# A two-layer attention and FFN kernel: the keys turned through the score banks, the output projections in two halves, both q projections ahead of the weighting

## Chip, cores and metric

The kernel is one program on one core of a Trainium2 chip. The metric is the device time of one execution in microseconds (us). Names of engines: PE is the matrix engine (TensorE), PEld its weight loads, DVE is VectorE, ACT is ScalarE, POOL is GpSimd.

## What is computed

The input x is 16 sequences of 64 rows of 512 numbers, in f32. Four blocks are added onto it, in this order:

```
x = x + xattn0(layernorm(x), ctx)   # 32 q heads, 8 kv heads, rotary positions, softmax over 64 keys
x = x + int_ffn(layernorm(x))       # 512 -> 1376 -> 512, rounded like int8
x = x + xattn1(layernorm(x), ctx)   # 32 q heads, 8 kv heads, keys = context and x (128), q and k normed by RMS
x = x + quant_ffn(layernorm(x))     # two 512x512 products on values rounded to 8 bits
```

Both attentions are of this shape, with (in the second) a norm of q and k in place of the rotation:

```
q = x @ Wq; k = c @ Wk; v = c @ Wv          # four q heads share one kv head
p = softmax(q @ k.T / sqrt(128) (+ mask))
x += (p @ v) @ Wo
```

## The kernel before

All four blocks are written by hand: each engine has its own program in a `block`, the order of the calls is the order of the work, and counting semaphores tie the engines together. The change touches the function `attention`, which runs twice: as `att0` (rope is true, 64 keys for each sequence) and as `att1` (rope is false, 128 keys).

**Precision.** Products with weights are taken as three matmuls of rounded parts (hi*hi, lo*hi, hi*lo), by `split_product` at line 70. Nearly all matmul rows of the trace are of that line.

**Units and slots.** An attention is 32 units u = 4g + n: kv head g (0 to 7) and n from 0 to 3, where n // 2 is the half of the sequences and n % 2 the pair of q heads (out of four). The loop over u is the spine of every engine's program. One pass is called a slot here. On PE a slot has these pieces:

- `scores(u)` (line 552 in att0, 555 in att1) into the banks `sco`;
- the filling work, `filling(g, n)`: for even n four output projections `project` of an earlier half (12 matmuls each), for odd n the joint k and v projections `kv_job` of the coming half (two in att0, four in att1);
- `turn(u)` (line 570): the softmax weights are turned into the banks `att`; it waits for POOL's `normalise(u)` (line 956);
- `q_job(u + 2, 0)` and `q_job(u + 2, 1)`: the q projections of the unit after the next, 12 matmuls each;
- `weigh(u)` (585 or 595): the turned weights times V, into two `att` banks; ACT rounds these (`round_out`, 882) and DVE takes the rest (`out_low`, 758), which counts the semaphore `out_drained`; `project` reads both parts;
- behind an odd unit `turn_keys` (534): the keys of the next half are turned, one bank in att0 and two in att1, and copied by ACT (`copy_keys`, 849) to `k_cols`, which the next `scores` reads. So slots with odd n are called key slots here. The even ones are out slots.

**Banks.** PE's results have eight banks: four `proj` in a ring, two `sco`, two `att`. The jobs in `att` are numbered in order (`number_att`), and a job takes the bank of the job before the last. A turned key therefore stands in a bank in which an output of `weigh` was, and waits until DVE has drained it (`att_room`).

**The order of the q jobs.** `early_q(u)` decides it: where it is true (att0 with odd u, and u < 2), both q jobs of the slot stand in front of `weigh`. Elsewhere `turn` comes first, one q job stands between `turn` and `weigh`, and the other behind `weigh` (and, in att1, behind `turn_keys`):

```
                if early_q(u):
                    q_job(u + 2, 0)
                turn(u)
                if rope and keys_after(u):
                    turn_keys(*keys_after(u))
                q_job(u + 2, 1 if early_q(u) else 0)
                weigh(u)
                if not rope and keys_after(u):
                    turn_keys(*keys_after(u))
                if not early_q(u):
                    q_job(u + 2, 1)
```

The last two units stand behind the loop, with the last eight output projections. POOL takes the low parts of the weights (142), the rotations of att0 (942), the scaling of the keys in att1 (950) and `normalise` (956). The weights come by DMA, 256 KB each.

Of the kernel before, what the change touches and what calls it, by code (L numbers as in the profile page):

```python
# [63 lines left out]
def split_product(eng, out, terms, more=False, first=True):  # L64


    n = 0
    for lhs_hi, lhs_lo, rhs_hi, rhs_lo in terms:
        for a, b in ((lhs_hi, rhs_hi), (lhs_lo, rhs_hi), (lhs_hi, rhs_lo)):
            last = eng.matmul(out, a, b, start=(first and n == 0), stop=(n == 3 * len(terms) - 1))  # L70
            n += 1
    return last
# [260 lines left out]
def attention(nc, st, tag, rope, weights, mask=None):  # L333
# [45 lines left out]
    for i in range(TKH):  # L379
        number_att("key", 0, 0, i)  # L380
    for u in range(UNITS):
# [7 lines left out]
        new_keys = (g, 1) if n == 1 else (g + 1, 0) if n == 3 and g + 1 < NKV else None  # L389
        for i in range(TJ):  # L390
            number_att("turn", u, i)
        if rope and new_keys:
            number_att("key", *new_keys, 0)
        for i in range(2):
            number_att("out", u, i)
        if not rope and new_keys:
            for i in range(TKH):
                number_att("key", *new_keys, i)
# [7 lines left out]

    def early_q(u):
        return rope and u % 2 == 1 or u < 2

    with ExitStack() as ctx:  # L410
# [30 lines left out]
        out_rounded, out_drained = sem("out_rounded"), sem("out_drained")  # L441
        inverted, normed, v_copied = sem("inverted"), sem("normed"), sem("v_copied")
# [14 lines left out]
        def o_slice(tile, u, i):  # L457
            p, sel = u % 2, (slice(i, NBH, 2) if rope else slice(4 * i, 4 * i + 4))
            return tile[:, 2 * p:2 * p + 2, sel, :].rearrange("p g b s -> p b g s")

# [24 lines left out]
        def _(eng):  # L485
# [37 lines left out]
            def turn_keys(g, h):  # L523
                for i in range(TKH):
# [4 lines left out]
                    turned, out = att_room("key", g, h, i)  # L529
                    need(eng, turned_copied, turned)  # L530
                    need(eng, out_drained, out)
                    bank = att_bank("key", g, h, i)
                    for c in range(4):
                        last = eng.transpose(bank[:, c * P:(c + 1) * P], k_rows[:, 4 * i + c], st.ident[:])
                    last.then_inc(att_full, 1)

            def scores(u):
# [5 lines left out]
                eng.wait_ge(turned_copied, turned_by["key", g, h, TKH - 1] + 1)  # L543
# [55 lines left out]
            def project(g, h, t):  # L599
                job = proj_job["out", g, h, t]  # L600
                eng.wait_ge(w_split, weights.ready(g, C_O + GROUP - 1))
                eng.wait_ge(out_drained, 2 * (4 * g + 2 * h + 2))
                need(eng, proj_drained, job - 3)
                split_product(eng, proj[job % 4][:], [
                    (o_hi[:, a, 2 * t:2 * t + 2, :], o_lo[:, a, 2 * t:2 * t + 2, :], w_hi[:, C_O + a], w_lo[:, C_O + a])
                    for a in range(GROUP)]).then_inc(proj_full, 1)

            def fill(what):
                kv_job(*what[1:]) if what[0] == "kv" else project(*what[1:])
# [12 lines left out]
            for u in range(UNITS - 2):  # L622
                work = filling(*divmod(u, 4))
                scores(u)
# [17 lines left out]
            project(g, 0, 0)  # L642
            q_sums(u + 1)
            project(g, 0, 1)
            project(g, 0, 2)
            scores(u + 1)
            turn(u)
            project(g, 0, 3)
            weigh(u)
            turn(u + 1)  # L650
            weigh(u + 1)
            for t in range(4):
                project(g, 1, t)

        @block.vector
        def _(eng):
# [129 lines left out]
            for u in range(UNITS - 2):  # L786
# [11 lines left out]
                if early_q(u):  # L798
                    take_q(u + 2, 1)
                out_low(u)  # L800
                if not early_q(u):
# [801 lines left out]
```

## Time and profile before

| | us |
|---|---|
| median of 3 runs | 1729.88 (1729.61 to 1732.37) |
| the profiled execution, its own time | 1730.62 |
| its span in the trace | 1728.8 |
| att0, slots 2 to 29 | 497.90 |
| att1, slots 0 to 29 | 743.71 |

The mean granted clock of PE is 0.952 of full speed. The span of the trace begins with the first instruction and ends with the last; the profiled execution's own time is 1.8 us longer. The stretches of the two attentions are cut at the first matmul of `scores`, so that one slot reaches from one `scores` to the next. The order is att0 (about 50 to 617 us), the integer FFN, att1 (861 to 1645 us), the quantised FFN. "Idle before" in a row is the time in which the engine stood still just ahead of the instruction, with what released it.

### The profile page before, as it was taken

What the parts mean: (1) busy time and instruction counts of PE and PEld (TensorE: products, weight loads), DVE (VectorE), ACT (ScalarE), POOL (GpSimd) and SP (SyncE); (2) the same over time, 40 slices, a digit from 0 to 9 for tenths busy, and PEclk for the clock granted to TensorE, in tenths of its full rate; (3) what the DMA queues carried; (4) which work ended last, traced back from release to release, by engine and by line L of the source; (5) the groups of instructions that cost most, each with busy time, mean ns of one, the idle gap of its engine ahead of it and who ended that gap; (6) DMA issues with size and microseconds to landing.
All of it is one profiled execution on the core that took longest, in us unless ns stands there. A gap on an engine that the chain in (4) does not pass through costs nothing. (4 is left out here: it accounts for less than half of the span.)

```text
span 1728.8 us, 28639 instructions
## 1 busy us (share of the span) xinstructions
PE 1534.0 (89%) x11533; PEld 1306.1 (76%) x11536; DVE 973.3 (56%) x1998; ACT 600.6 (35%) x1424; POOL 564.6 (33%) x458
## 2 busy tenths in 40 slices
PE   4899999999999879987799999999999999999826
PEld 4788887888787668865688888888888788888723
DVE  6656666566655646648555444544544454455487
ACT  3212222122221224422353443435344343534345
POOL 3535444353433325522222221312222131222045
PEclk9999999999999989998899999999999999999958
DMA  5101111011110012201110010101001010100021
GB/s 163 48 27 50 35 40 37 25 58 30 38 38 25 1 55 73 69 1 57 54 38 25 25 38 1 57 6 38 26 25 38 11 52 2 38 26 1 1 73 49
DMA packets 81229, 64.43 MB, mean 37 GB/s; under 512 B 7280, under 2 KB 66928, under 8 KB 81104
## 3 DMA queue, kind: packets, MB, share of 16 engines
q1 hardware_dynamic: 80240, 62.47, 12.4%
q8 instruction: 90, 1.47, 0.4%
q14 instruction: 35, 0.29, 0.1%
q10 hardware_dynamic: 864, 0.20, 0.1%
HBM read 60.56 MB, written 2.10 MB: 36 GB/s over the span
## 5 line engine op out<-in xcount | busy, mean ns | idle before, releaser
L956 POOL TENSOR_TENSOR att_probs<-att_probs,att_total 128x512 f32<-128x512 f32 x64 | 82.9, 1295 | 566.6 <-DVE att_total L748 428.8
L142 POOL TENSOR_TENSOR att_w_lo<-att_w_raw,att_w_hi 128x512 fp32r<-128x512 f32 x160 | 205.5, 1309 | 160.2 <-ACT att_w_hi L137 160.2
L70 PE MATMUL att_proj<-att_w_hi,kv_hi 128*128 128x256 f32 x768 | 223.9, 291 | 8.7 <-PEq L223 8.6
L70 PE MATMUL att_proj<-att_w_hi,att_o_hi 128*128 128x512 f32 x512 | 205.2, 401 | 24.2 <-issue 24.2
L70 PE MATMUL att_proj<-att_w_hi,kv_lo 128*128 128x256 f32 x768 | 218.9, 285 | 0.0
L70 PE MATMUL att_proj<-att_w_lo,kv_hi 128*128 128x256 f32 x768 | 218.8, 285 | 0.0
L70 PE MATMUL att_proj<-kv_hi,att_w_hi 128*128 128x512 f32 x512 | 217.3, 424 | 0.0
L764 DVE TENSOR_TENSOR x_rows<-att_proj,x_rows 128x512 f32<-128x512 f32 x128 | 88.6, 692 | 220.4 <-PE att_proj L70 220.4
L70 PE MATMUL att_proj<-kv_hi,att_w_lo 128*128 128x512 f32 x512 | 206.9, 404 | 0.0
L70 PE MATMUL att_proj<-kv_lo,att_w_hi 128*128 128x512 f32 x512 | 206.8, 404 | 0.0
L70 PE MATMUL att_proj<-att_w_hi,att_o_lo 128*128 128x512 f32 x512 | 201.0, 392 | 0.0
L70 PE MATMUL att_proj<-att_w_lo,att_o_hi 128*128 128x512 f32 x512 | 200.6, 392 | 0.0
L70 PEld LDWEIGHTS att_proj<-att_w_hi,kv_hi 128*128 128x128 f32 x768 | 149.0, 194 | 10.8 <-issue 9.4
L871 ACT ACTIVATE att_probs_t<-att_att 128x512 f32<-128x512 f32 x96 | 54.0, 596 | 279.3 <-PE att_att L570 278.4
L70 PEld LDWEIGHTS att_proj<-att_w_hi,kv_lo 128*128 128x128 f32 x768 | 149.1, 194 | 0.0
L70 PEld LDWEIGHTS att_proj<-att_w_lo,kv_hi 128*128 128x128 f32 x768 | 149.0, 194 | 0.0
L861 ACT ACTIVATE att_probs<-att_sco,att_low,att_q_rms 128x128 f32<-128x128 f32 x256 | 113.3, 461 | 62.7 <-DVE att_low L728 62.7
L70 PEld LDWEIGHTS att_proj<-att_w_hi,att_o_hi 128*128 128x128 f32 x512 | 96.9, 189 | 45.6 <-issue 26.2
L942 POOL TENSOR_TENSOR att_q_cols<-att_turn_a,att_turn_b 128x512 f32<-128x512 f32 x64 | 86.2, 1346 | 125.5 <-DVE att_turn_b L681 125.5
L70 PEld LDWEIGHTS att_proj<-kv_lo,att_w_hi 128*128 128x128 f32 x512 | 100.3, 196 | 22.7
L70 PEld LDWEIGHTS att_proj<-kv_hi,att_w_hi 128*128 128x128 f32 x512 | 101.6, 198 | 19.3
L882 ACT ACTIVATE att_o_hi<-att_att 128x512 fp32r<-128x512 f32 x128 | 72.9, 597 | 120.4 <-PE att_att L585 101.3
(153 smaller groups left out, 2950.8 us busy)
## 6 DMA issues: line engine op xcount, KB each, us to landing
att_w_raw<-in_wq SPq DMA_DIRECT2D x64, 256.0 KB, 2.9
att_w_raw<-in_wo SPq DMA_DIRECT2D x64, 256.0 KB, 2.7
ln_stage<-in_ctx_t SPq DMA_DIRECT2D x8, 512.0 KB, 5.0
att_w_raw<-in_wk SPq DMA_DIRECT2D x16, 256.0 KB, 3.5
att_w_raw<-in_wv SPq DMA_DIRECT2D x16, 256.0 KB, 3.4
ffn_w_raw<-in_gate_t SPq DMA_DIRECT2D x10, 256.0 KB, 2.9
ffn_w_raw<-in_up_t SPq DMA_DIRECT2D x10, 256.0 KB, 3.2
ffn_w_raw<-in_down_t SPq DMA_DIRECT2D x10, 256.0 KB, 3.0
```

What stands on the lines that cost most here:

```text
L70: last = eng.matmul(out, a, b, start=(first and n == 0), stop=(n == 3 * len(terms) - 1))
L142: eng.tensor_tensor(self.lo[:, chunk], self.raw[:, n % RAW_SLOTS], raw(self.hi[:, chunk]), ALU.subtract)\
L764: eng.tensor_tensor(st.x[:, row], proj[job % 4][:], st.x[:, row], ALU.add).then_inc(proj_drained, 1)
L861: ins = eng.activation(probs[:, u % 2, b], sco[(u * SJ + i) % 2][:, c * KL:(c + 1) * KL], ACT.Exp, bias=low[:, u % 2, one], scale=q_rms[:, ...
L871: eng.activation(probs_t[:, slot], att_bank("turn", u, i)[:], ACT.Copy).then_inc(turned_copied, 1)
L882: eng.activation(o_slice(o_hi, u, i), bank, ACT.Copy).then_inc(out_rounded, 1)
L942: eng.tensor_tensor(dst, a, b, ALU.add).then_inc(rotated, 1)
L956: eng.tensor_tensor(probs[:, u % 2, 0:n], probs[:, u % 2, 0:n], total[:, u % 2, 0:n].unsqueeze(2).broadcast_to([P, n, KL]), ALU.mult)\
```

## The change

It has four parts, for both attentions.

- The keys are turned into the `sco` banks, where the next scores will go, in place of the `att` banks. The semaphores `keys_full` and `keys_copied` are new. The turning waits until the scores of all earlier units are drained (`sco_drained`), and `scores` waits for `keys_copied`. The `att` banks then hold `turn` and `weigh` alone.
- `project(g, h, t)` is cut into two half sums, p = 0 and p = 1, of six matmuls each, over two of the four heads. Half p waits for the outputs of the unit 4g + 2h + p alone. At the start of an out slot the order is t0 p0, t1 p0, t0 p1.
- `early_q` is gone. Every slot ends with q, `turn`, q, `turn_keys` (if any), `weigh`; ACT and DVE follow: both `square_q`, then `copy_keys`, then `round_out` on ACT, both `take_q` and then `out_low` on DVE.
- Behind the loop the first halves of the last four projections stand ahead of the last `turn`, the second halves at the end.

```
-            def project(g, h, t):
+            def project(g, h, t, p):
                 job = proj_job["out", g, h, t]
-                eng.wait_ge(w_split, weights.ready(g, C_O + GROUP - 1))
-                eng.wait_ge(out_drained, 2 * (4 * g + 2 * h + 2))
-                need(eng, proj_drained, job - 3)
-                split_product(...for a in range(GROUP)]).then_inc(proj_full, 1)
+                eng.wait_ge(w_split, weights.ready(g, C_O + 2 * p + 1))
+                eng.wait_ge(out_drained, 2 * (4 * g + 2 * h + p + 1))
+                if p == 0:
+                    need(eng, proj_drained, job - 3)
+                last = split_product(... for a in (2 * p, 2 * p + 1)], first=(p == 0), last=(p == 1))
+                if p == 1:
+                    last.then_inc(proj_full, 1)
...
             def turn_keys(g, h):
+                need(eng, sco_drained, SJ * key_unit(g, h))
                 for i in range(TKH):
...
-                    turned, out = att_room("key", g, h, i)
-                    need(eng, turned_copied, turned)
-                    need(eng, out_drained, out)
-                    bank = att_bank("key", g, h, i)
+                    bank = key_bank(g, h, i)
...
-                    last.then_inc(att_full, 1)
+                    last.then_inc(keys_full, 1)
...
             for u in range(UNITS - 2):
-                work = filling(*divmod(u, 4))
                 scores(u)
-                fill(work[0])
+                work = filling(*divmod(u, 4))
+                fill_first(work)
                 q_sums(u + 1)
-                for what in work[1:]:
-                    fill(what)
-                if early_q(u):
-                    q_job(u + 2, 0)
+                fill_rest(work)
+                q_job(u + 2, 0)
                 turn(u)
-                if rope and keys_after(u):
+                q_job(u + 2, 1)
+                if keys_after(u):
                     turn_keys(*keys_after(u))
-                q_job(u + 2, 1 if early_q(u) else 0)
                 weigh(u)
-                if not rope and keys_after(u):
-                    turn_keys(*keys_after(u))
-                if not early_q(u):
-                    q_job(u + 2, 1)
...
             weigh(u)
+            for t in range(4):
+                project(g, 1, t, 0)
             turn(u + 1)
             weigh(u + 1)
             for t in range(4):
-                project(g, 1, t)
+                project(g, 1, t, 1)
```

What PE has in a row at the end of a key slot of att1 (u = 9), before. In the names, `att1_` is the second attention, and the number behind a tile is its bank. Rows of line 70 with `kv1_hi` and 512 columns open a q job; the 11 rows that follow each are left out:

```order
L70 MATMUL att1_proj3<-kv1_hi,att1_w_hi 128x512 [waits att1_proj_drained,att1_w_split]
...
L595 MATMUL att1_att0<-att1_probs_t,att1_v_rows 128x128 [waits att1_turned_copied,att1_v_copied]
...
L595 MATMUL att1_att1<-att1_probs_t,att1_v_rows 128x128 [waits att1_turned_copied]
...
L534 MATMUL att1_att0<-ident,att1_k_rows 128x128 [waits att1_out_drained,att1_k_scaled]
...
L534 MATMUL att1_att1<-ident,att1_k_rows 128x128 [waits att1_out_drained,att1_k_scaled]
...
L70 MATMUL att1_proj0<-kv1_hi,att1_w_hi 128x512 [waits att1_proj_drained,att1_w_split]
...
L555 MATMUL att1_sco0<-att1_k_cols,att1_q_cols 128x128 [waits att1_sco_drained,att1_turned_copied,att1_proj_drained]
```

The same place of the changed program, from the q job behind `turn` to the first halves of the output projections (rows with `att1_o_hi`):

```order
L70 MATMUL att1_proj0<-kv1_hi,att1_w_hi 128x512 [waits att1_proj_drained,att1_w_split]
...
L529 MATMUL att1_sco0<-ident,att1_k_rows 128x128 [waits att1_k_scaled,att1_sco_drained]
...
L529 MATMUL att1_sco1<-ident,att1_k_rows 128x128 [waits att1_k_scaled]
...
L590 MATMUL att1_att0<-att1_probs_t,att1_v_rows 128x128 [waits att1_turned_copied,att1_v_copied]
...
L590 MATMUL att1_att1<-att1_probs_t,att1_v_rows 128x128 [waits att1_turned_copied]
...
L550 MATMUL att1_sco0<-att1_k_cols,att1_q_cols 128x128 [waits att1_sco_drained,att1_keys_copied,att1_proj_drained]
...
L550 MATMUL att1_sco1<-att1_k_cols,att1_q_cols 128x128 [waits att1_sco_drained]
...
L70 MATMUL att1_proj1<-att1_w_hi,att1_o_hi 128x512 [waits att1_proj_drained,att1_out_drained,att1_w_split]
...
L70 MATMUL att1_proj2<-att1_w_hi,att1_o_hi 128x512 [waits att1_proj_drained,att1_out_drained,att1_w_split]
...
L70 MATMUL att1_proj1<-att1_w_hi,att1_o_hi 128x512 [waits att1_out_drained,att1_w_split]
```

The turning of the keys no longer waits for `out_drained` and stands ahead of `weigh`; no q job is left between `weigh` and `scores`. A second bank is opened before the first sum is closed.

What ACT has in a row at the same place, before:

```order
L871 ACTIVATE att1_probs_t<-att1_att0 128x512 [waits att1_att_full]
L871 ACTIVATE att1_probs_t<-att1_att1 128x512 [waits att1_att_full]
L842 ACTIVATE att1_squares<-att1_proj3 128x8x64 [waits att1_proj_full]
L882 ACTIVATE att1_o_hi<-att1_att0 128x4x2x64 [waits att1_proj_full,att1_att_full]
L882 ACTIVATE att1_o_hi<-att1_att1 128x4x2x64 [waits att1_att_full]
L849 ACTIVATE att1_k_cols<-att1_att0,qk_norm 128x512 [waits att1_att_full]
L849 ACTIVATE att1_k_cols<-att1_att1,qk_norm 128x512 [waits att1_att_full]
L842 ACTIVATE att1_squares<-att1_proj0 128x8x64 [waits att1_proj_full]
```

And now:

```order
L878 ACTIVATE att1_probs_t<-att1_att0 128x512 [waits att1_att_full]
L878 ACTIVATE att1_probs_t<-att1_att1 128x512 [waits att1_att_full]
L849 ACTIVATE att1_squares<-att1_proj3 128x8x64 [waits att1_proj_full]
L849 ACTIVATE att1_squares<-att1_proj0 128x8x64 [waits att1_proj_full]
L856 ACTIVATE att1_k_cols<-att1_sco0,qk_norm 128x512 [waits att1_keys_full]
L856 ACTIVATE att1_k_cols<-att1_sco1,qk_norm 128x512 [waits att1_keys_full]
L889 ACTIVATE att1_o_hi<-att1_att0 128x4x2x64 [waits att1_proj_full,att1_att_full]
L889 ACTIVATE att1_o_hi<-att1_att1 128x4x2x64 [waits att1_att_full]
```

Both squares and both copies of the keys now stand ahead of the rounding of the outputs.

## Rows read from the trace of the kernel before

**Rows 1.** The page, part 1: busy us, share of the span, instructions.
```profile
PE 1534.0 (89%) x11533; PEld 1306.1 (76%) x11536; DVE 973.3 (56%) x1998; ACT 600.6 (35%) x1424; POOL 564.6 (33%) x458
```

**Rows 2.** Waits of all engines in att0: engine line waited for: us, times, longest.
```profile
PE att_proj L70 <- issue: 20.7, 15, 1.4
```

**Rows 3.** The same in att1, 850 to 1640 us.
```profile
PE att_att L534 <- DVE att_o_lo L758: 47.8, 15, 3.5
```

**Rows 4.** Stretches of slots: us; busy (instructions) PE, PEld, DVE, ACT, POOL; granted clock.
```profile
79.97:577.87 497.90, 478.34 (x3530) 401.15 (x3528) 301.34 (x505) 118.05 (x224) 215.37 (x182) 1.00 0.12 36
860.69:1604.40 743.71, 693.94 (x6074) 615.88 (x6072) 362.06 (x921) 310.34 (x885) 169.51 (x134) 0.96 0.09 26
860.69:877.63 16.94, 16.74 (x177) 15.24 (x176) 8.98 (x33) 9.38 (x27) 1.55 (x1) 1.00 0.01 2
1025.48:1054.97 29.49, 26.14 (x233) 24.17 (x232) 12.78 (x37) 11.01 (x32) 3.58 (x3) 0.88 0.01 2
...
1076.72:1103.80 27.08, 23.73 (x234) 22.04 (x233) 13.82 (x37) 14.04 (x38) 9.89 (x9) 1.00 0.14 40
1103.80:1125.55 21.75, 21.75 (x177) 18.39 (x176) 12.55 (x24) 9.18 (x26) 7.75 (x7) 1.00 0.25 74
293.34:314.42 21.08, 19.68 (x126) 15.66 (x124) 11.67 (x18) 6.63 (x12) 9.54 (x8) 1.00 0.18 51
```

**Rows 5.** PE in order of time, end of att1's key slot 7.
```profile
1043.50 1.95 PE L595 MATMUL att_att<-att_probs_t,att_v_rows 128*128 128x128 f32 x16
1048.73 1.94 PE L534 MATMUL att_att<-ident,att_k_rows 128*128 128x128 f32 x8 [3.28 <-DVE att_o_lo L758]
```

**Rows 6.** DVE, POOL and ACT in order of time, same place.
```profile
1047.90 1.28 DVE L758 TENSOR_TENSOR att_o_lo<-att_att,att_o_hi 128x512 fp32r<-128x512 f32 x2
...
1043.80 2.04 POOL L950 TENSOR_TENSOR att_k_rows<-att_k_rows,att_k_rms 128x512 f32<-128x512 f32 x2 [4.03 <-DVE att_k_rms L216]
...
1049.85 0.69 ACT L849 ACTIVATE att_k_cols<-att_att,qk_norm 128x512 f32<-128x512 f32 x1 [3.77 <-PE att_att L534]
```

**Rows 7.** PE, then DVE, in order of time, att0's slot 15 and the start of 16.
```profile
321.36 0.40 PE L70 MATMUL att_proj<-kv_hi,att_w_hi 128*128 128x512 f32 x1
...
324.12 0.60 PE L570 MATMUL att_att<-ident,att_probs 128*128 128x128 f32 x4
...
324.91 0.48 PE L70 MATMUL att_proj<-kv_hi,att_w_hi 128*128 128x512 f32 x1
...
327.81 1.16 PE L585 MATMUL att_att<-att_probs_t,att_v_rows 64*128 64x128 f32 x16
328.91 1.15 PE L552 MATMUL att_sco<-att_k_cols,att_q_cols 128*64 128x64 f32 x32
331.44 0.47 PE L70 MATMUL att_proj<-att_w_hi,att_o_hi 128*128 128x512 f32 x1 [1.38 <-issue]
...
330.05 1.29 DVE L758 TENSOR_TENSOR att_o_lo<-att_att,att_o_hi 128x512 fp32r<-128x512 f32 x2
```

**Rows 8.** POOL, then PE, in att0's key slot 17, whose scores start at 349.99.
```profile
353.52 2.99 POOL L142 TENSOR_TENSOR att_w_lo<-att_w_raw,att_w_hi 128x512 fp32r<-128x512 f32 x2
357.23 0.74 POOL L942 TENSOR_TENSOR att_k_rows<-att_turn_a,att_turn_b 128x256 f32<-128x256 f32 x1 [0.71 <-DVE att_turn_b L669]
358.06 1.04 POOL L956 TENSOR_TENSOR att_probs<-att_probs,att_total 128x512 f32<-128x512 f32 x1
...
359.68 0.60 PE L570 MATMUL att_att<-ident,att_probs 128*128 128x128 f32 x4
```

**Rows 9.** PE in order of time, att1, the end of slot 0.
```profile
875.85 1.95 PE L595 MATMUL att_att<-att_probs_t,att_v_rows 128*128 128x128 f32 x16
877.63 1.95 PE L555 MATMUL att_sco<-att_k_cols,att_q_cols 128*128 128x128 f32 x16
```

**Rows 10.** PE in order of time, the last turn of att0 and of att1.
```profile
598.33 1.11 PE L570 MATMUL att_att<-ident,att_probs 128*128 128x128 f32 x4 [3.96 <-POOL att_probs L956]
...
1627.85 1.97 PE L570 MATMUL att_att<-ident,att_probs 128*128 128x128 f32 x8 [5.22 <-POOL att_probs L956]
```

More of the change, by code:

```diff
@@ L61, with split_product @@
     pass
-def split_product(eng, out, terms, more=False, first=True):
+def split_product(eng, out, terms, first=True, last=True):
     n = 0
@@ L69, in split_product @@
         for a, b in ((lhs_hi, rhs_hi), (lhs_lo, rhs_hi), (lhs_hi, rhs_lo)):
-            last = eng.matmul(out, a, b, start=(first and n == 0), stop=(n == 3 * len(terms) - 1))
+            ins = eng.matmul(out, a, b, start=(first and n == 0), stop=(last and n == 3 * len(terms) - 1))
             n += 1
-    return last
+    return ins
 def raw(ap):
@@ L378, in attention @@
     number("q", 1, 1)
-    for i in range(TKH):
-        number_att("key", 0, 0, i)
     for u in range(UNITS):
@@ L597, in weigh, with fill_first, fill_rest @@
                     last.then_inc(att_full, 1)
-            def project(g, h, t):
+            def project(g, h, t, p):
                 job = proj_job["out", g, h, t]
-                eng.wait_ge(w_split, weights.ready(g, C_O + GROUP - 1))
-                eng.wait_ge(out_drained, 2 * (4 * g + 2 * h + 2))
-                need(eng, proj_drained, job - 3)
-                split_product(eng, proj[job % 4][:], [
-                    (o_hi[:, a, 2 * t:2 * t + 2, :], o_lo[:, a, 2 * t:2 * t + 2, :], w_hi[:, C_O + a], w_lo[:, C_O + a])
-                    for a in range(GROUP)]).then_inc(proj_full, 1)
-            def fill(what):
-                kv_job(*what[1:]) if what[0] == "kv" else project(*what[1:])
+                eng.wait_ge(w_split, weights.ready(g, C_O + 2 * p + 1))
+                eng.wait_ge(out_drained, 2 * (4 * g + 2 * h + p + 1))
+                if p == 0:
+                    need(eng, proj_drained, job - 3)
+                last = split_product(eng, proj[job % 4][:], [
+                    (o_hi[:, a, 2 * t:2 * t + 2, :], o_lo[:, a, 2 * t:2 * t + 2, :], w_hi[:, C_O + a], w_lo[:, C_O + a])
+                    for a in (2 * p, 2 * p + 1)], first=(p == 0), last=(p == 1))
+                if p == 1:
+                    last.then_inc(proj_full, 1)
+            def fill_first(work):
+                if work[0][0] == "kv":
+                    kv_job(*work[0][1:])
+                    return
+                project(*work[0][1:], 0)
+                project(*work[1][1:], 0)
+                project(*work[0][1:], 1)
+            def fill_rest(work):
+                for i, what in enumerate(work[1:]):
+                    if what[0] == "kv":
+                        kv_job(*what[1:])
+                        continue
+                    if i:
+                        project(*what[1:], 0)
+                    project(*what[1:], 1)
             for j in range(KVH):
@@ L797, in _ @@
                 take_q(u + 2, 0)
-                if early_q(u):
-                    take_q(u + 2, 1)
+                take_q(u + 2, 1)
                 out_low(u)
-                if not early_q(u):
-                    take_q(u + 2, 1)
             u, g = UNITS - 2, NKV - 1
```

43 lines of the change are left out of this document (18 added, 25 removed).

## The prediction, made before the changed kernel was run

> **What bounds the kernel now.** Part 1 of the page comes first: PE is busy for 89% of the span, no other engine for more than 56% [rows 1]. So what counts is where PE stands still or runs slowly. I then read the waits of PE by stage, and then the order of time around each.
>
> In att0 one wait repeats: 15 times 1.4 us, 20.7 us in all, ahead of an output projection [rows 2]. The order of time shows which: `scores(16)` starts at 328.91, takes 1.09 us (the step from `weigh` to `scores`, 327.81 to 328.91, is as long), and the first projection starts at 331.44, because `out_low` on DVE runs from 330.05 to 331.34 [rows 7]. Start to start the loss is 1.44 us, a little more than the modelled 1.38. It stands in every out slot from 2 to 30: the key slot ahead of it has `weigh` last. An out slot takes 21.08 us, and the granted clock is 1.00 over all of slots 2 to 29 [rows 4].
>
> In att1 PE waits for DVE's `out_low` before it turns keys: 47.8 us in 15 places [rows 3]. `weigh` starts at 1043.50; 16 matmuls of 0.106 us end at 1045.20; the turning starts at 1048.73, when DVE, which began `out_low` only at 1047.90, has drained the first bank [rows 5, 6]. The loss is 3.53 us. Then comes the second price: the 8 transposes take 1.94 us, where 8 of att0 take 0.79 (324.12 to 324.91) [rows 7], since the clock has fallen to the lower of its two levels (1.2 GHz, not 2.4). Slot 7 takes 29.49 us at clock 0.88, slot 9, without the lower level, 27.08 at 1.00 [rows 4]. Out slots take 21.75 at 1.00, with PE busy throughout. What the clock costs in all comes out of the same rows: slot 0 of 16.94, slot 1 of at most 21.3 (slot 0, 0.8 for its keys, 3.5 of stall), and 14 pairs of 27.08 + 21.75 make 721.9; the stretch took 743.71. So 21.8 us are the clock's.
>
> **The change, part by part.** The sum is made against the profiled execution's own time, 1730.62 us, which is 0.74 above the median.
>
> *Keys in the score banks, ahead of `weigh`.* The wait for `out_drained` goes. What the turning waits for instead: the scores drained (the softmax of the same slot needs them, done before `turn`), and the keys scaled. In slot 7 POOL scales them from 1043.80 to 1045.84 [rows 6]. `weigh` began at 1043.50, behind one q job; now the filling is followed by q, turn, q, so the turning begins one q job (2.76 us) later, at 1046.3: 0.4 us to spare. Each clean key slot then costs 27.08 - 3.53 = 23.55 us. Behind the transposes stand `weigh` and `scores`, and `scores` needs the copies. With T the start of the turning, ACT squares q until T + 0.9 (0.2 us of lag and 0.69, as its copy of a bank takes) and copies twice in 0.69: T + 2.3. PE comes to `scores` at T + 0.8 + 1.8 = T + 2.6 (`weigh` takes 1.78, rows 9). In att0 it is one copy, T + 1.35 against T + 0.4 + 1.1 = T + 1.5 [rows 6, 7, 9]. Both are hidden, by 0.3 and 0.15 us; I price them at nothing and keep 0.3 us in 30 slots, 9 us, for the upper end.
>
> *Half sums.* In att0 `out_low` ends 2.43 us after `weigh` does (331.34 against 328.91) [rows 7]. The first matmul that needs it now stands behind `scores` and two halves: 1.1 + 2 x 1.38 = 3.9 us. So the 1.44 us go, with 1.4 to spare. In att1 no q job stands between `weigh` and the projections any more, so the wait could be new there. In slot 7 `weigh` would end at 1046.3 + 0.8 + 1.8 = 1048.9, and the second half of t0 comes 1.8 + 2.8 us later, at 1053.5. DVE ends `out_low` at 1049.18, plus a `take_q` of 0.7 that now stands before it: 1049.9. Hidden by 3.5 us. The number of matmuls is the same, and sums in two banks at once cost nothing that the rows show.
>
> *Both q jobs ahead of `weigh`.* `weigh` and `scores` become neighbours in 28 more slots. Each change from the large to the small products and back costs a little: the q job right behind the filling takes 321.36 to 324.12 = 2.76 us, the one behind small ones 324.91 to 327.81 = 2.90 [rows 7]. I take 0.14 in att0 and 0.1 in att1. DVE begins the next scores behind `out_low`, about where it began them before.
>
> It has a cost in att0. With n = 0 POOL splits four chunks after ACT has rounded them behind `round_out`. In slot 17 that ended at 356.51, 6.5 us after `scores` began at 349.99, and `normalise` ran from 358.06 to 359.10, just ahead of `turn` at 359.68 [rows 8]. `scores` now begins one q job earlier against that chain. From the end of `weigh`: three roundings on ACT at 0.6, 1.8; four splits and a rotation of the same size on POOL at 1.3 to 1.5 (2.99 for two), some 6.9; the rotation of keys 0.74 and 1.04 for `normalise`: 10.5 us, against 9.7 at which `turn` arrives (359.68 - 349.99). ACT and POOL overlap a little, so I take a new wait of 0.5 us in 7 slots, 3.5 us; bounds 0 and 1.0 each.
>
> *The tails.* PE stood idle 3.96 and 5.22 us before the last turns, for POOL [rows 10]. The four first halves (5.5 us) fill that, but they need `out_low` of the unit just weighed, so a stall of 2 to 3.5 us appears ahead of them. I take 2 us gained in each; bounds 0 and 9.2 together.
>
> *The clock.* In att0 idle stretches of 1.44 us never brought the lower level in 28 slots. If att1 has no idle of 3.5 us left I expect the full clock there too. The 21.8 us are then gone as well.
>
> **The sum.** att1, slots 0 to 29, was 743.71. Now slot 0: 16.94 as before; slot 1 is slot 0 plus 8 transposes, 17.8 (rounded up); 14 out slots of 21.65; 14 key slots of 23.45. That makes 666.1, so 77.6 saved. att0: 14 x (1.44 + 0.14) + 1.44 - 3.5 = 20.1. Tails 4. In all 101.7: 1730.62 - 101.7 = 1628.9, and 1628.2 as a median.
>
> **A rule against it.** Rows 9 show `weigh` and `scores` as neighbours at full speed, 16 matmuls in 1.78 us, twice over: 3.5 us of small products without a fall. In a key slot the turning now stands before them, 4.4 us. The Trainium skill, TensorE: Matmul & The Clock Gate, Part 4: PE-mode transpose, says that a transpose doesn't count as PE-busy in the way a matmul does. By that rule the turned keys lengthen a quiet stretch, and the lower level stays in the key slots. No row has turning, weighting and scores in a row, so none refutes it; rival 1 is what it would come to.
>
> **The rivals.**
> 1. *The clock keeps falling in key slots*, because 4.4 us of small products work as the idle stretch did. For it: the new length. Against it: rows 9, and clock 1.00 in att0, where `weigh`, `scores` and 1.44 us of idle stood together. Price: the 21.8 us of now, giving 1650; with slot 7's 29.49 - 27.08 = 2.4 in each of 15 slots 36, giving 1664.
> 2. *Small waits take the place of the large one*: the copies or the scaled keys come later than the margins of 0.15 to 0.4 us. At 0.8 us in 30 slots, 24 us: 1652.
> 3. *Slower.* Turning now stands in front of `weigh`, so a late key holds `weigh`, and with it `round_out`, `out_low` and the projections. POOL would have to deliver 101.7 / 30 = 3.4 us behind PE in each key slot to eat up the gain, that is 3.8 later than in slot 7; from there it decides. At 4 us: 120 us, 1748. Against it: nothing ahead of the scaling on DVE or POOL moves.
> 4. *No change*: the stalls only move, as to the second half of t0. Margins of 1.4 and 3.5 us speak against it. About 1730.
>
> **Chances.** The forecast 0.76, rival 1 0.10, rival 2 0.10, rival 3 0.02, rival 4 0.02. So faster 0.96, same 0.02, slower 0.02; 0.2% is about what a measurement of this kernel can tell. The lower end: tails 9.2 (-5), no wait in slot 17's kind (-3.5), and the waits for `normalise` in the out slots gone too (-3): 1617. The upper end: tails 0 (+4), 1.0 us in that kind (+3.5), copies late (+9), and half a step of rival 1: 1648.
>
> **What would show it.** Right: no row of PE waiting for `out_low` ahead of turned keys; key slots of att1 near 23.5 and out slots near 21.65; out slots of att0 near 19.5; granted clock 1.00 in both; a small wait of `turn` for POOL in att0's slots 5, 9, 13 and so on. Wrong: clock below 0.98 in att1 (rival 1); PE waiting for ACT's copies or POOL's keys (rival 2), or for `out_low` in the second half of t0 (rival 4).

## The result and the profile after

The changed kernel takes 1623.77 us, the median of 4 executions (1622.98 to 1625.15); the kernel before took 1729.74 on the same chip (4 executions, 1728.78 to 1732.37). The ratio is 0.9386, with a 95% interval of 0.937 to 0.9402: faster by 6.1%. The forecast was 1628 (1617 to 1648), 4 us too high. The profiled execution took 1622.98 us with a span of 1621.2, against 1730.62 and 1728.8 before. (Of the four executions of the experiment q_order_only below, one of 1729.89 us had a mean clock of 0.89 where the others had 0.96 to 0.97; its figures there leave it out.)

Part 1 of the page after, beside [rows 1]: PE's busy time fell by 39 us although it executes the same number of matmuls, and its share rose from 89 to 92%.

```profile
PE 1495.1 (92%) x11533; PEld 1287.9 (79%) x11536; DVE 980.7 (60%) x1998; ACT 596.4 (37%) x1424; POOL 564.6 (35%) x458
```

The stretches after, with the columns of [rows 4] (from and to, length; busy PE, PEld, DVE, ACT, POOL with instructions; granted clock; DMA share; GB/s). In order: slots 2 to 29 of att0, slots 0 to 29 of att1, att1's slot 0, one of its key slots and one of its out slots; then from att0 the out slot 16, and the key slots 17 and 19:

```profile
79.36:556.30 476.94, 473.71 (x3531) 403.47 (x3529) 299.74 (x505) 119.62 (x224) 214.69 (x182) 1.00 0.13 37
835.68:1498.51 662.83, 662.62 (x6073) 596.87 (x6072) 370.97 (x921) 304.70 (x885) 170.09 (x134) 1.00 0.10 29
835.68:852.62 16.94, 16.74 (x178) 15.26 (x177) 9.00 (x33) 9.38 (x27) 1.55 (x1) 1.00 0.00 1
1026.42:1049.56 23.14, 23.14 (x235) 21.92 (x234) 13.89 (x38) 12.76 (x36) 8.63 (x7) 1.00 0.16 46
1049.56:1071.31 21.75, 21.75 (x179) 18.47 (x178) 13.81 (x25) 10.12 (x28) 9.08 (x7) 1.00 0.25 74
317.50:336.73 19.23, 19.23 (x128) 15.81 (x126) 10.54 (x17) 2.32 (x4) 3.62 (x3) 1.00 0.00 1
336.73:351.91 15.18, 14.72 (x132) 12.97 (x130) 10.67 (x21) 5.65 (x11) 10.44 (x9) 1.00 0.24 71
371.12:385.63 14.51, 14.51 (x132) 13.04 (x130) 10.26 (x21) 3.57 (x7) 6.79 (x7) 1.00 0.12 37
```

The second row is the main reading: PE busy for 662.62 of 662.83 us at clock 1.00, where [rows 4] had 693.94 of 743.71 at 0.96. The two long rows of waits [rows 2, 3] are gone. What PE still waits for in att0 (75 to 560 us) is one row; in att1 (830 to 1500 us) it is 0.2 us, once:

```profile
PE att_att L565 <- POOL att_probs L958: 3.2, 7, 0.5
```

Where the 107.6 us between the two profiled spans came from, by the starts of the slots in the two traces: att1's slots 0 to 29 80.9 (743.71 - 662.83), att0's slots 2 to 29 21.0 (497.90 - 476.94), the stretch from att0's slot 30 to att1's slot 0 3.4 (282.82 to 279.38), what follows att1's slot 29 1.7 (124.4 to 122.7), and 0.6 ahead of slot 2.

PE in order of time in the changed kernel, att1's key slot 11 (the counterpart of [rows 5]), and behind it ACT's row of copies and DVE's first `out_low`:

```profile
1091.79 1.03 PE L529 MATMUL att_sco<-ident,att_k_rows 128*128 128x128 f32 x8
1092.66 1.95 PE L590 MATMUL att_att<-att_probs_t,att_v_rows 128*128 128x128 f32 x16
1094.45 1.95 PE L550 MATMUL att_sco<-att_k_cols,att_q_cols 128*128 128x128 f32 x16
1096.15 0.48 PE L70 MATMUL att_proj<-att_w_hi,att_o_hi 128*128 128x512 f32 x1
...
1092.48 1.26 ACT L856 ACTIVATE att_k_cols<-att_sco,qk_norm 128x512 f32<-128x512 f32 x2
...
1094.38 0.69 DVE L768 TENSOR_TENSOR att_o_lo<-att_att,att_o_hi 128x512 fp32r<-128x512 f32 x1
```

Turned keys, `weigh` and `scores` fill 1091.79 to 1096.15, 4.36 us, each starting as the one before ends. The copies end at 1093.74, 0.7 us ahead of the scores that read them. POOL had scaled the keys at 1091.68, only 0.1 us ahead of the turning where the prediction had 0.4, but the q job ahead of the turning takes its usual 2.82 us, so nothing waited. `out_low` starts 0.07 us before `scores` do and nothing on PE asks for it yet.

### The profile page after: what moved, and what is told of

Same layout as the page of the kernel before. It is cut to its first block and busy times, and to the rows that moved or that the text cites. A ratio compares the mean times of both kernels' runs of the same rounds, so it can differ in the third digit from the quotient of the medians.

```text
span 1621.2 us, 28750 instructions
## 1 busy us (share of the span) xinstructions
PE 1495.1 (92%) x11533; PEld 1287.9 (79%) x11536; DVE 980.7 (60%) x1998; ACT 596.4 (37%) x1424; POOL 564.6 (35%) x458
## 5 line engine op out<-in xcount | busy, mean ns | idle before, releaser
L958 POOL TENSOR_TENSOR att_probs<-att_probs,att_total 128x512 f32<-128x512 f32 x64 | 82.9, 1296 | 478.3 <-DVE att_total L758 359.4
L70 PE MATMUL att_proj<-kv_hi,att_w_hi 128*128 128x512 f32 x512 | 207.2, 405 | 0.0
L70 PE MATMUL att_proj<-kv_lo,att_w_hi 128*128 128x512 f32 x512 | 201.6, 394 | 0.0
L70 PE MATMUL att_proj<-kv_hi,att_w_lo 128*128 128x512 f32 x512 | 201.0, 393 | 0.0
L774 DVE TENSOR_TENSOR x_rows<-att_proj,x_rows 128x512 f32<-128x512 f32 x128 | 88.6, 692 | 182.1 <-PE att_proj L70 182.1
L944 POOL TENSOR_TENSOR att_q_cols<-att_turn_a,att_turn_b 128x512 f32<-128x512 f32 x64 | 89.4, 1397 | 101.7 <-DVE att_turn_b L691 101.7
L698 DVE COPY att_k_rows<-att_proj 128x256 f32<-128x256 f32 x64 | 27.2, 425 | 145.2 <-ACT att_v_rows L842 145.2
L70 PEld LDWEIGHTS att_proj<-kv_lo,att_w_hi 128*128 128x128 f32 x512 | 96.7, 189 | 21.5
L70 PEld LDWEIGHTS att_proj<-att_w_lo,att_o_hi 128*128 128x128 f32 x512 | 96.6, 189 | 20.9
```

Of the source, the lines that this page charges most:

```text
L70: ins = eng.matmul(out, a, b, start=(first and n == 0), stop=(last and n == 3 * len(terms) - 1))
L698: eng.tensor_copy(k_rows[:, 2 * j:2 * j + 2], bank[:, :, 0]).then_inc(proj_drained, 1)
L774: eng.tensor_tensor(st.x[:, row], proj[job % 4][:], st.x[:, row], ALU.add).then_inc(proj_drained, 1)
L944: eng.tensor_tensor(dst, a, b, ALU.add).then_inc(rotated, 1)
L958: eng.tensor_tensor(probs[:, u % 2, 0:n], probs[:, u % 2, 0:n], total[:, u % 2, 0:n].unsqueeze(2).broadcast_to([P, n, KL]), ALU.mult)\
```

## The experiments

All savings are against the kernel before on the same chip (medians 1731.53 for the first four runs, 1730.08 for the next three, 1730.93 for the last two). The diffs show the core of each.

### Each part alone

**banks_only** is the kernel before with the keys turned in the banks of the scores, still behind `weigh`, with semaphores of their own.

```diff
             def turn_keys(g, h):
+                need(eng, sco_drained, SJ * key_unit(g, h))
...
-                    need(eng, out_drained, out)
-                    bank = att_bank("key", g, h, i)
+                    bank = key_bank(g, h, i)
```

> Kernel before, with one part of the change: the keys are turned into the score banks, at the places and in the order of before; whole projections, q jobs as before. Theory A (each part removes its own stall; the wait of the turned keys for the drained outputs is the cause of att1's loss, and that idle stretch the cause of the lower clock): key slots of att1 near 23.4 us with granted clock 1.00, out slots 21.75, att0 unchanged with its 15 stalls of 1.4 us; in all 1730 - 15 x 3.5 - 22 = 1655, within 1650 to 1662. Theory B (the order of the q jobs is what frees PE, the bank is a detail): key slots stay above 25 us and the time above 1690.

Measured: 1658.60 (1658.12 to 1660.95), ratio 0.958 (0.9562 to 0.9599), 72.9 us saved. Slots 2 to 29 of att1 in one row, then one of its key slots, then PE's waits in att0:

```profile
896.92:1533.15 636.23, 635.25 (x5712) 565.69 (x5713) 339.76 (x854) 286.62 (x825) 159.57 (x126) 1.00 0.10 29
1055.11:1078.76 23.65, 23.58 (x233) 22.01 (x232) 13.77 (x37) 13.93 (x38) 9.88 (x9) 1.00 0.16 46
...
PE att_proj L70 <- issue: 19.3, 14, 1.4
```

In these slots of att1 no stall and no lower level is left; att0's waits stay. The stall cost 27.08 - 23.65 = 3.43 us in a key slot without the lower level, where the prediction had 3.53.

**halves_only** is the kernel before with the output projections as half sums.

```diff
-                eng.wait_ge(out_drained, 2 * (4 * g + 2 * h + 2))
...
+                eng.wait_ge(out_drained, 2 * (4 * g + 2 * h + p + 1))
...
+                last = split_product(eng, proj[job % 4][:], [
...
-                    for a in range(GROUP)]).then_inc(proj_full, 1)
...
+                    for a in (2 * p, 2 * p + 1)], first=(p == 0), last=(p == 1))
```

> Kernel before, with one part of the change: the projections as two half sums, started t0 p0, t1 p0, t0 p1; keys and q jobs as before; behind the loop both halves stand together, so the tails are those of before. Theory A: the 15 stalls of 1.44 us in att0 go, out slots there near 19.64 us, att1 unchanged; 1730 - 21.6 = 1708, within 1704 to 1712. Theory B (without the q order the halves only move the stall): above 1722.

Measured: 1706.01 (1703.23 to 1707.09), ratio 0.9852 (0.9835 to 0.987), 25.5 us saved. Att0's slots 2 to 29, att1's slots 2 to 29, and PE's waits in att1:

```profile
79.61:557.80 478.19, 477.93 (x3531) 401.15 (x3529) 301.41 (x505) 118.11 (x224) 215.93 (x182) 1.00 0.13 37
876.36:1577.03 700.67, 653.67 (x5713) 579.26 (x5714) 339.46 (x853) 288.69 (x825) 159.48 (x126) 0.97 0.09 26
...
PE att_att L534 <- DVE att_o_lo L777: 47.6, 15, 3.5
```

Att0 loses its 1.44 us waits (497.90 to 478.19, 19.7 us), att1 keeps its 15 (most of them 3.28 us, the longest 3.5) and the lower level (clock 0.97). That level came in fewer of its slots than in the kernel before: slots 2 to 29 of att1 took 700.67 for 706.39, so 5.7 us between the two profiles are not the half sums' but the clock's.

**q_order_only** is the kernel before with `early_q` true for every slot: both q jobs stand ahead of `weigh`.

```diff
     def early_q(u):
-        return rope and u % 2 == 1 or u < 2
+        return True
```

> Kernel before, with both q jobs ahead of the weighting in every slot; the keys stay in the att banks and, in att1, behind the weighting; whole projections. Theory A: att1's key slots keep a stall for the drained outputs, shorter (1.7 us as slot 1 has it in the kernel before), and get a second one, of scores for the copies of the keys (1.2 us), near 26.4 us, part of them at the lower clock; att0 gains 0.14 to 0.36 us in 14 slots; 1705 to 1730. Theory B: below 1660.

Measured: 1695.47 (1693.79 to 1697.01), ratio 0.9785 (0.9762 to 0.9807), 36.1 us saved: below what the first theory expected and far above the second, so both missed. A key slot and the waits of PE in att1 (855 to 1590 us):

```profile
1066.64:1092.56 25.92, 23.66 (x235) 21.94 (x233) 15.06 (x39) 13.59 (x38) 8.63 (x7) 1.00 0.15 42
...
PE att_att L534 <- DVE att_o_lo L758: 21.9, 15, 1.7
PE att_sco L555 <- issue: 12.4, 15, 0.8
```

The stall of 3.3 us has become two, 1.43 us ahead of the turned keys and 0.82 ahead of `scores` for the copies, and with that the lower level no longer follows the stalls from slot 3 on (clock 1.00). That was not foreseen. By the starts of the slots, att1's slots 2 to 29 went from 706.4 to 669.5 us; 14 key slots shorter by 27.08 - 25.92 are 16.2 of these 36.9, and the other 20.7 are the clock's. Att0 gains nothing in sum: its out slots are 0.43 shorter (20.65), seven key slots 0.94 longer for the wait that the prediction put there.

**stall_filled** is the kernel before with the second q job moved between `weigh` and the turned keys, so that it fills part of the stall; ACT squares it ahead of copying the keys. The banks and the whole projections stay, and so do the small products, of which now the turned keys and `scores` stand together, where it was `weigh` and the turned keys.

```diff
                 weigh(u)
-                if not rope and keys_after(u):
-                    turn_keys(*keys_after(u))
                 if not early_q(u):
                     q_job(u + 2, 1)
+                if not rope and keys_after(u):
+                    turn_keys(*keys_after(u))
```

> Kernel before, where in att1 the q job behind the turned keys stands between the weighting and the turned keys. The bank and its wait stay. It tells what brings the lower clock. Theory A (a long idle stretch): the 3.5 us are cut to 0.7 us, a second stall of about 1.5 us appears ahead of scores, since the copies of the keys are no longer covered; key slots near 25.8 us, all at granted clock 1.00: 1730 - 14 x 1.3 - 22 = 1690, within 1684 to 1698. Rival (small products, weighting and turned keys, bring it): the lower level stays in most key slots, clock of att1 near 0.96, time above 1705.

Measured: 1689.37 (1688.29 to 1691.02), ratio 0.9757 (0.974 to 0.9775), 42.2 us saved. The last two small pieces and their waits in a key slot, and the slots 2 to 29 of att1:

```profile
1086.11 1.22 PE L534 MATMUL att_att<-ident,att_k_rows 128*128 128x128 f32 x8 [0.54 <-DVE att_o_lo L758]
1088.16 0.57 PE L555 MATMUL att_sco<-att_k_cols,att_q_cols 128*128 128x128 f32 x3 [0.82 <-issue]
...
898.39:1561.17 662.78, 642.43 (x5712) 567.14 (x5713) 341.89 (x854) 288.42 (x826) 159.41 (x126) 1.00 0.10 27
```

The clock is 1.00 in the mean with 0.54 and 0.82 us idle; two stretches at the lower level were left, at the start of slot 2 (behind 1.59 and 0.82 us idle in slot 1) and in slot 20 (behind 0.77 and 0.82 in slot 19). In q_order_only all the small products of a key slot stand in a row, as in the changed kernel, and the level stayed up from slot 3 on. Together the two say that in att1 it was mostly the long idle stretch that brought the lower level, not the small products around it.

### The parts together

**banks_and_halves** is the changed kernel with the q jobs and the tails in their old places.

```diff
-                q_job(u + 2, 0)
+                if early_q(u):
+                    q_job(u + 2, 0)
                 turn(u)
-                q_job(u + 2, 1)
...
                 weigh(u)
+                if not rope and keys_after(u):
+                    turn_keys(*keys_after(u))
+                if not early_q(u):
+                    q_job(u + 2, 1)
```

> The changed kernel without its q order and its tails: keys in the score banks and half sums, q jobs and the place of the turned keys as in the kernel before. It prices the third part. Theory A: slots of att1 within 0.3 us of the changed kernel's (23.1 and 21.75), out slots of att0 near 19.6 where the changed kernel has 19.2, key slots of att0 all at 14.5 (no wait for normalise), tails as before; 1624 + 14 x 0.4 - 7 x 0.7 + about 4 to 6 for the tails = 1629, within 1625 to 1636. Theory B (the q order carries the gain): above 1660.

Measured: 1635.29 (1634.55 to 1635.69), ratio 0.9454 (0.9441 to 0.9467), 94.8 us saved. It lies inside the range and 6 us above its point, so order and tails are worth some 11 us (94.8 against 106.0 saved), where the prediction gave them 5.3 (4 for the tails, 4.8 for order, less 3.5 for the new wait in att0). By the starts of the slots, of 12.6 us between the two profiled spans 8.3 are in att1's slots 0 to 29, 1.2 in att0's slots 2 to 29, 2.7 in the tails and 0.4 ahead of slot 2. A key slot of att1 and an out slot of att0, then PE and POOL around `turn` in that key slot:

```profile
1032.70:1056.38 23.68, 23.61 (x233) 22.02 (x232) 13.80 (x37) 13.93 (x38) 9.90 (x9) 1.00 0.16 45
318.85:338.51 19.66, 19.64 (x126) 15.65 (x124) 11.28 (x18) 5.16 (x10) 4.09 (x4) 1.00 0.00 1
...
1046.71 0.28 PE L70 MATMUL att_proj<-att_w_lo,kv_hi 128*128 128x256 f32 x1
1047.06 1.09 PE L568 MATMUL att_att<-ident,att_probs 128*128 128x128 f32 x8
...
1052.52 1.26 PE L532 MATMUL att_sco<-ident,att_k_rows 128*128 128x128 f32 x8
1053.53 0.47 PE L70 MATMUL att_proj<-kv_hi,att_w_hi 128*128 128x512 f32 x1
...
1045.45 1.55 POOL L973 TENSOR_TENSOR att_probs<-att_probs,att_total 128x512 f32<-128x512 f32 x1 [6.32 <-DVE att_total L765]
```

Matmuls of 256 columns follow each other here every 0.12 us, so `turn` could have begun at 1046.83; it began at 1047.06, when POOL's `normalise` had ended at 1047.00. That is a wait of 0.23 us, of which the rows show 0.07 as idle, since the last matmul's row ends only at 1046.99; the view of waits has no row for it. The kernel before had it too: its `normalise` ended at 1091.01 and `turn` started at 1091.06.

```profile
1089.46 1.55 POOL L956 TENSOR_TENSOR att_probs<-att_probs,att_total 128x512 f32<-128x512 f32 x1 [6.33 <-DVE att_total L748]
...
1091.06 1.09 PE L570 MATMUL att_att<-ident,att_probs 128*128 128x128 f32 x8
```

In the changed kernel `turn` arrives a q job later and the wait is gone: `normalise` of slot 11 ends at 1085.60, 2.6 us ahead of `turn` at 1088.18. The rest of the 0.54 us per key slot goes with fewer changes between large and small products: turned keys 1.01 here (1052.52 to 1053.53) and 0.87 in the changed kernel (1091.79 to 1092.66), the first q job 2.76 for 2.85, `turn` 0.79 for 0.85. In att1's out slots a q job gains 0.09 as well, but `weigh`, now right ahead of `scores`, takes 1.78 for 1.70, so nothing is left.

Att0's out slots had the same hidden wait. In banks_and_halves the last projection matmul of slot 16 starts at 330.74, the next could at 330.97, and `turn` starts at 331.14, when `normalise` had ended at 331.09: 0.18 us, the same in every out slot from 2 to 28, and the same in the kernel before (306.64, 307.05, and 306.99 for the end). In the changed kernel the step is 0.23 and `normalise` is done 2.6 us earlier.

### What was left in the changed kernel

The 0.46 us that PE waits for `normalise` in seven key slots of att0 was forecast, and the rows of POOL in slot 17 of the changed kernel, whose `scores` start at 336.72, show its cause: `normalise` (L958) stands behind two splits and a rotation, and ends at 346.97, just ahead of `turn` at 347.02.

```profile
347.02 0.66 PE L565 MATMUL att_att<-ident,att_probs 128*128 128x128 f32 x4 [0.46 <-POOL att_probs L958]
...
342.72 2.54 POOL L142 TENSOR_TENSOR att_w_lo<-att_w_raw,att_w_hi 128x512 fp32r<-128x512 f32 x2
345.24 0.73 POOL L944 TENSOR_TENSOR att_k_rows<-att_turn_a,att_turn_b 128x256 f32<-128x256 f32 x1
345.93 1.04 POOL L958 TENSOR_TENSOR att_probs<-att_probs,att_total 128x512 f32<-128x512 f32 x1
```

**splits_later** is the changed kernel with two of the four splits moved, in att0, into the next slot and behind its `normalise`.

```diff
                     rotate(*what)
+                if n == 1 and rope:
+                    split_w(g, C_O + 2, C_O + 3)
...
-                if n == 0:
+                if n == 0 and not rope:
                     split_w(g, C_O + 2, C_O + 3)
```

> The changed kernel, where in att0 POOL takes the split of the last two output chunks one slot later, behind normalise and the rotation of the keys. The wait of turn for POOL in slots 5, 9 to 29 (0.46 us idle, slots of 15.18 in place of 14.51) should go: 7 x 0.67 = 4.7 us, 1619; within 1617 to 1621. If the cause of those 0.67 us is another (DVE late, not the splits), they stay and the time is 1624.

Measured: 1617.79 (1615.91 to 1618.80), ratio 0.9351 (0.9339 to 0.9364). Att0's slots 2 to 29, and slot 17 (15.18 in the changed kernel); the view of PE's waits from 76 to 560 us is empty:

```profile
76.14:548.57 472.43, 472.43 (x3530) 403.98 (x3528) 299.75 (x505) 119.64 (x224) 215.27 (x182) 1.00 0.13 38
...
331.58:346.09 14.51, 14.51 (x130) 13.04 (x128) 10.66 (x21) 5.65 (x11) 10.51 (x9) 1.00 0.25 74
```

The wait cost 476.94 - 472.43 = 4.5 us in these slots, up to 0.67 in each of seven, for 0.46 of recorded idle. Slot 2 starts 3.2 us earlier as well (79.36 to 76.14): 2.5 of them are slot 1, where `turn` waits 1.72 us in place of 2.61 and the lower level no longer follows. Of these 7.7 the medians show 6.0. In the profiled execution of splits_later the clock fell twice in att0's tail (567 to 571 and 577 to 581 us), which in that of the changed kernel it did not, and the stretch from att0's slot 30 to att1 took 282.1 us for 279.4.

**splits_and_tail** is splits_later with the first half of the last projection ahead of the last `weigh` but one, and its second half behind it, to fill the stall ahead of the last halves.

```diff
             turn(u)
-            for p in range(2):
-                project(g, 0, 3, p)
+            project(g, 0, 3, 0)
             weigh(u)
+            project(g, 0, 3, 1)
```

> As splits_later, and behind the loop the last projection of the first half is cut: one half sum ahead of the weighting, one behind it, where PE waited 2.05 us in att0 and 3.52 in att1 for the drained outputs. The half (1.4 us) fills part of the wait: 2 x 1.4 = 2.8 us less than splits_later, 1616; if the weighting then waits for the copy of the turned weights (turn to weighting has 1.4 us in place of 2.8), up to 0.3 us less gain each; within 1614 to 1619.

Measured: 1618.98 (1617.32 to 1619.48), ratio 0.9357 (0.9344 to 0.9369): no gain over splits_later, against what was expected. In att1's tail PE still waited 3.50 us. DVE's `out_low` there, PE's row behind the wait, and two rows of DVE in att0's tail:

```profile
1514.64 1.29 DVE L768 TENSOR_TENSOR att_o_lo<-att_att,att_o_hi 128x512 fp32r<-128x512 f32 x2 [0.65 <-ACT att_o_hi L889]
...
1516.03 0.47 PE L70 MATMUL att_proj<-att_w_hi,att_o_hi 128*128 128x512 f32 x1 [3.50 <-issue]
...
564.14 0.69 DVE L774 TENSOR_TENSOR x_rows<-att_proj,x_rows 128x512 f32<-128x512 f32 x1 [2.28 <-PE att_proj L70]
...
565.48 1.27 DVE L768 TENSOR_TENSOR att_o_lo<-att_att,att_o_hi 128x512 fp32r<-128x512 f32 x2
```

The two tails differ. In att0 the adding of that very projection (L774) stands ahead of `out_low` (L768) on DVE, which follows it without an idle row of its own: PE's filler postponed what PE waited for, and PE waited 2.75 us where it had waited 2.05. In att1 DVE had done the adding and waited 0.65 us more for ACT, whose eight exponentials stand ahead of `round_out`; they set the time with the filler and without it (the halves start 10.85 us after the last `scores` in both kernels), so the filler could gain nothing.

**tail_reordered** is splits_and_tail with both changed: `out_low` ahead of the adding on DVE, `round_out` ahead of the exponentials on ACT.

```diff
-            add_out(g, 0, 3)
             out_low(u)
+            add_out(g, 0, 3)
...
-            exponentials(u + 1)
             round_out(u)
+            exponentials(u + 1)
```

> splits_and_tail, whose cut of the last projection brought nothing. Theory A: the halves behind the last weighting but one wait for out_low, and out_low was held by what stands ahead of it: on DVE the sum of that last projection (add_out), which the cut made later; on ACT, in att1, the eight exponentials of unit 31 (3.9 us) ahead of the rounding. Here out_low stands ahead of add_out on DVE, and the rounding ahead of the exponentials on ACT. The halves should start 1.4 us earlier in att0 and about 3 us earlier in att1: 4.5 us less than splits_and_tail, 1614, within 1612 to 1617. Theory B: the end of each attention is set by normalise of unit 31, which the rounding now delays; then no more than 1 us is gained, 1618.

Measured: 1612.42 (1612.05 to 1614.82), ratio 0.9321 (0.9308 to 0.9334). In the same place:

```profile
1509.59 1.29 DVE L768 TENSOR_TENSOR att_o_lo<-att_att,att_o_hi 128x512 fp32r<-128x512 f32 x2 [2.78 <-ACT att_o_hi L889]
...
1510.98 0.47 PE L70 MATMUL att_proj<-att_w_hi,att_o_hi 128*128 128x512 f32 x1 [2.11 <-issue]
```

The halves start 0.6 us earlier in att0 and 1.4 in att1, counted from the last `scores`; 1.4 and 3 were expected. That the time still fell by 6.6 us, where 4.5 were expected, goes with the clock: the waits of 2.11 us in both tails were followed by no lower level, where splits_and_tail had it from 567.6 to 571.0, from 577.8 to 584.7 and from 1516.5 to 1519.9.

**changed_again**, the changed kernel once more, ran beside it:

> The changed kernel unchanged, on the same chip and in the same rounds as tail_reordered, so that the two can be compared: 1624 us, within 1622 to 1626.

Measured: 1622.21 (1621.16 to 1624.01), ratio 0.9368 (0.9356 to 0.9381). On one chip, then, the reordered version, which has the later splits too, is 9.8 us (0.6%) faster than the changed kernel and 118.5 faster than the one before; it beats both.

## Why the prediction was right, step by step

**The stalls.** Both mechanisms were as described. The keys in other banks took the 3.5 us from att1 (banks_only), the half sums took the 1.44 us from att0 (halves_only, 19.7 us over slots 2 to 29 for the 20.2 of 14 x 1.44), and neither touched the other's waits. The new places of their waits did not bind: the key copies had 0.7 us to spare where 0.3 was forecast, and there is no row of waiting for `out_low` behind the first halves. Rivals 2, 3 and 4 fall with that.

**The clock.** The 21.8 us came back; att1 runs at 1.00. (The starts of the slots before give a little more: slot 1 took 20.37 us, not the 21.3 that the prediction allowed it, since it stalled 1.66 and 0.82 us and not 3.5; so 22.8 were the clock's.) Rival 1 falls: in each of the 14 key slots PE does 4.36 us of small products in a row, turned keys first, without the lower level. So the rule of the Trainium skill that stood against the change (TensorE: Matmul & The Clock Gate, Part 4: PE-mode transpose, that a transpose doesn't count as PE-busy in the way a matmul does) brought nothing here; no run tells whether the chip counts them so. q_order_only and stall_filled show what mattered most, the idle stretch.

**The parts do not add up.** Alone they save 72.9, 25.5 and 36.1 us, 134.5 together; all at once, and with the tails, 106.0. Two things are counted twice. One is the clock: whatever shortens att1's stall, by banks, by order or by filling it, brings back most of the same 22 us, and the first to come gets them. The other is the stall itself, of which order alone takes 16.2 us that the banks take anyway: alone, order saves 36.9 us in att1's slots 2 to 29, on top of banks and halves 7.1 (635.59 to 628.49). Banks and halves, of which only the first touches att1's stall, add up well (98.4 against 94.8 together).

**Att1's slots.** Forecast 666.1, measured 662.83. Key slots 23.14 for 23.45; out slots 21.75 for 21.65; slot 0 16.94 as said; slot 1 17.41 for 17.8. The step that failed in size is the one on changes between large and small products, "0.14 in att0 and 0.1 in att1". Order is worth 23.68 - 23.14 = 0.54 us in a key slot and nothing in an out slot (21.72 in banks_and_halves, 21.75 after). Of the 0.54, 0.23 is a wait that stands in no term of the prediction: no row listed `turn` of the kernel before as waiting, but its start lay 0.05 us behind the end of `normalise`. The 0.31 that is left is what the 0.1 should have been.

**Att0's slots.** Slots 2 to 29 were to save 14 x 1.58 - 3.5 = 18.6 us and saved 21.0. Out slots 19.23 for 19.5: 0.43 from order (19.66 to 19.23) for 0.14. Of the 0.43, 0.18 is the hidden wait for `normalise`, which the prediction had only in the lower end of its range (3 us; 14 x 0.18 is 2.5), and 0.25 is the same mis-sized term. Against it, the new wait for POOL came where it was forecast, in the seven key slots with n = 1, at 0.67 us for 0.5.

**The tails.** Forecast 2 us each. With slot 30 itself taken off (10.90 to 9.46), 3.4 - 1.4 = 2.0 and 1.7 are left. These are small differences that hang on one execution: in changed_again the clock fell behind the same 2.05 us wait, and the stretch from att0's slot 30 to att1 took 282.0 us, 0.8 less than before in place of 3.4. Against banks_and_halves, which has the half sums and the old tails, the new tails are worth 1.9 and 0.8. The stall of "2 to 3.5 us" ahead of the four halves is there, and the last `turn` no longer waits. PE in the changed kernel, att0's tail and then att1's:

```profile
573.41 0.47 PE L70 MATMUL att_proj<-att_w_hi,att_o_hi 128*128 128x512 f32 x1 [2.05 <-issue]
...
1520.25 0.47 PE L70 MATMUL att_proj<-att_w_hi,att_o_hi 128*128 128x512 f32 x1 [3.52 <-issue]
...
1521.83 0.63 PE L70 MATMUL att_proj<-att_w_lo,att_o_hi 128*128 128x512 f32 x1
...
1527.43 1.03 PE L565 MATMUL att_att<-ident,att_probs 128*128 128x128 f32 x8
```

**The range.** Its upper end doesn't come out of its own terms: 1628.2 + 4 + 3.5 + 9 is 1644.7, and half of rival 1's 21.8 us would make it 1655.6, not 1648. The result lies at the other side of the point and doesn't depend on it.

**The sum.** Saved against the forecast: att1 80.9 for 77.6, att0 with slot 30 22.4 for 20.1, tails 3.7 for 4, and 0.6 ahead of slot 2 for nothing: 107.6 for 101.7. The mechanisms were right. What was missed is mostly the order priced too low, against which att1's out slots (1.4 us) and att0's new wait (1.0) went the other way.

## What to carry to other kernels

When PE turns, weighs or adds in a bank that another engine still has to drain, look for banks whose reader is done by then for another reason; the scores of the same slot were such banks, and that edit alone gave two thirds of the gain. Split a sum at the operand that comes late, so that the halves which need it stand last. Fill a stall only after looking at what the filler makes the late engine do first: in att0's tail of splits_and_tail the filler queued its own consumer ahead of the instruction that PE waited for, and in att1's another engine's work set the time. And compare the start of each PE step with the end of its producer, since a wait of 0.2 us in every slot was in no row of the view of waits.

## What the runs showed of the hardware

**An idle stretch and the clock.** Each count here is of one profiled execution. Stalls of 3.3 to 3.5 us brought TensorE to the lower of its two levels in 10 of the 14 key slots 3 to 29 of att1 before, in 9 of 14 in halves_only, and after the 3.52 us in the changed kernel's last tail: there the matmuls of 512 columns, 0.23 us apart, are 0.43 apart from 1521.4 to 1524.4. In att0's slot 1, 2.6 us of waiting did so in all eight runs that have it, and 1.7 in none of the three others. Stalls of 1.4 us alone did so nowhere (15 places each in att0 of the kernel before, banks_only, q_order_only and stall_filled). Two short ones, a few small products apart, did seldom: 1.43 to 1.45 and 0.82 us in none of 13 key slots of q_order_only, 0.54 and 0.82 in none of 13 of stall_filled, but 1.6 and 0.82 behind slot 1 in both. Scores of slot 2 in q_order_only, where 16 take 1.95 at full speed:

```profile
898.34 1.23 PE L534 MATMUL att_att<-ident,att_k_rows 128*128 128x128 f32 x8 [1.62 <-DVE att_o_lo L758]
900.39 3.37 PE L555 MATMUL att_sco<-att_k_cols,att_q_cols 128*128 128x128 f32 x16 [0.82 <-issue]
```

The fourteenth key slot of each, slot 19, has a longer first wait and turns the order around. In q_order_only 1.66 and 0.82 us left the clock at full speed (first two rows), in stall_filled 0.77 and 0.82 did not (third row):

```profile
1329.27 1.23 PE L534 MATMUL att_att<-ident,att_k_rows 128*128 128x128 f32 x8 [1.66 <-DVE att_o_lo L758]
1331.32 2.02 PE L555 MATMUL att_sco<-att_k_cols,att_q_cols 128*128 128x128 f32 x16 [0.82 <-issue]
...
1323.97 3.29 PE L555 MATMUL att_sco<-att_k_cols,att_q_cols 128*128 128x128 f32 x16 [0.82 <-issue]
```

So the length alone doesn't decide it. Nor does the program: the same kernel waited 2.05 us in att0's tail both times it was profiled. The first time it went on at full speed (573.41 above; clock 1.00 from 556 to 590 us); in changed_again it fell, as the 0.63 shows:

```profile
572.35 0.47 PE L70 MATMUL att_proj<-att_w_hi,att_o_hi 128*128 128x512 f32 x1 [2.05 <-issue]
...
574.38 0.63 PE L70 MATMUL att_proj<-att_w_hi,att_o_lo 128*128 128x512 f32 x1
```

What decides between two such executions stays open.

**A recorded wait is less than the time lost.** In slot 17 of the changed kernel `turn` starts at 347.02, the matmul before it at 346.17. Such matmuls start every 0.23 us, so 0.62 is lost where the row says 0.46, and the slot is 0.67 longer than one without the wait (15.18, 14.51).
